# Sixteen units turned by DMA instead of eight, and ScalarE's codes issued up to eight units ahead

## The reference

```
layer 0:  P = softmax(x Wq (x Wk)^T + mask(adj));   x = layernorm(x + P (x Wv))
layer 1:  h = x W^T + b
          e[i, j] = leaky_relu(h[i] . a1 + h[j] . a2 + b_a, 0.2)
          A = softmax(where(adj > 0, e, -9e15));    x = layernorm(x + A h)
```

## Time and profile before

| | |
|---|---|
| median of three runs | 245.96 us (245.84 to 246.24) |
| the profiled execution | 246.06 us, span 244.3 us |
| busy: TensorE, VectorE, ScalarE, GpSimd | 227.7, 185.9, 154.6, 63.4 us |
| DMA | 73.85 MB, mean 302 GB/s, 385 GB/s in most slices up to 165 us |
| granted clock | 1.00 up to 239.6 us |

### The profile page before, as it was taken

The page is one execution under the profiler, slowest core; times in us unless marked ns, Lnnn a source line. Parts: engine busy times, 40 slices in busy tenths (PEclk is TensorE's granted clock), DMA queues, the critical chain, the costliest instruction groups (busy, mean ns, idle before and its releaser), DMA issues.

```text
span 244.3 us, 3945 instructions
## 1 busy us (share of the span) xinstructions
PE 227.7 (93%) x1445; PEld 127.0 (52%) x1445; DVE 185.9 (76%) x284; ACT 154.6 (63%) x182; POOL 63.4 (26%) x107
## 2 busy tenths in 40 slices
PE   3869999999999999999999999999999999999970
PEld 2745666455555556455555545565455555544550
DVE  1378788886998776979677787977877778899352
ACT  3287986989769977640789993710899991420041
POOL 3375578999500000003120000002300000042241
PEclk9999999999999999999999999999999999999996
DMA  5999999999999999999979999999489997310102
GB/s 149 367 383 370 385 386 387 384 386 387 384 387 386 385 387 386 385 384 386 349 167 362 387 396 395 387 386 369 137 295 343 389 256 147 66 51 15 43 3 91
DMA packets 52600, 73.85 MB, mean 302 GB/s; under 512 B 15457, under 2 KB 19810, under 8 KB 52578
## 3 DMA queue, kind: packets, MB, share of 16 engines
q1 hardware_dynamic: 52000, 73.43, 86.4%
q10 hardware_dynamic: 578, 0.13, 0.3%
HBM read 69.36 MB, written 2.10 MB: 293 GB/s over the span
## 4 chain that ended last, share of the span: by engine, by line
PE 85%; POOL 4%; ACT 4%; issue 2%; DMA 1%; DVE 1%; POOLq 0%; DVEq 0%; ACTq 0%
PE banks L1267 68%; PE banks L1218 9%; PE banks L1284 3%; ACT a L792 3%; PE banks L1156 2%; DMA x_sb<-in_x_dram 1%; PE banks L1171 1%; POOL f_parts L682 1%; PE banks L1142 1%; POOL feat L675 1%; POOL rstd L643 1%; POOL f_parts L680 1%; ACT xhat_st L756 0%; POOL xhat_st L648 0%; PE banks L1188 0%
## 5 line engine op out<-in xcount | busy, mean ns | idle before, releaser
L1267 PE MATMUL banks<-e_sb,f_parts 128*128 128x512 f16 (+1 forms) x786 | 183.3, 382 | 1.8 <-DVE e_sb L996 1.2
L984 DVE SCALAR_TENSOR_TENSOR e_sb<-R,cr_word,banks 128x1024 f32<-128x1024 f32 x108 | 133.5, 1275 | 23.5 <-PE banks L1218 20.6
L792 ACT ACTIVATE a<-a_sb,code_bias 128x2048 fp8e4<-128x2048 int32 x64 | 124.8, 1997 | 3.5 <-DMA a_sb<-in_adj_dram 3.0
L1267 PEld LDWEIGHTS banks<-e_sb,f_parts 128*128 128x128 f16 x786 | 72.9, 96 | 86.2 <-issue 1.7
L700 POOL TENSOR_TENSOR frstd<-frv,minus_half 128x4 f32<-128x4 f32 x7 | 8.0, 1149 | 156.5 <-DVE frv L1020 156.5
L1218 PEld LDWEIGHTS banks<-ident,a 128*128 128x128 f16 x432 | 28.2, 97 | 10.3 <-ACT a L792 0.5
L1218 PE MATMUL banks<-ident,a 128*128 128x128 f16 x432 | 32.5, 219 | 0.2 <-ACT a L792 0.2
L779 ACT COPY R<-banks 128x512 f32<-128x512 f32 x8 | 4.7, 587 | 31.7 <-PE banks L1171 31.7
L984 DVE SCALAR_TENSOR_TENSOR e_sb<-R,cr_word,x_sb 128x1024 f32<-128x1024 f32 x16 | 20.5, 1324 | 0.0
L808 ACT ACTIVATE junk<-y 128x128 f32<-128x128 f32 x28 | 8.3, 297 | 19.0 <-DVE y L1011 18.9
L1156 PE MATMUL banks<-m0c_um,x_tr 128*128 128x130 f32 x64 | 9.7, 299 | 1.4 <-ACT x_tr L752 0.7
(11 more groups left out here) (113 smaller groups left out, 108.7 us busy)
## 6 DMA issues: line engine op xcount, KB each, us to landing
a_sb<-in_adj_dram SPq DMA_DIRECT2D x128, 512.0 KB, 10.7
x_sb<-in_x_dram SPq DMA_DIRECT2D x8, 256.0 KB, 8.7
out_dram<-out_sb SPq DMA_DIRECT2D x8, 256.0 KB, 5.9
x_sb<-a SPq DMA_TRANSPOSE x8, 3.4
w_nat<-in_L_gnn_W_dram ACTq DMA_DIRECT2D x1, 64.0 KB, 2.6
wv<-in_L_gnn_Wv_dram ACTq DMA_DIRECT2D x1, 64.0 KB, 3.0
acol<-in_L_gnn_a_vec_dram SPq DMA_DIRECT2D x1, 1.0 KB, 3.1
bcol<-in_L_gnn_b_W_dram ACTq DMA_DIRECT2D x1, 0.5 KB, 2.9
```

The lines of the kernel that those rows point to most:

```text
L792: nc.scalar.activation(a_words[:, n % 2, k, :, Q * h:Q * (h + 1), :].rearrange("p e r x -> p r e x"), a_parts[:, m % SLOTS, :, :].rearrang ...
L984: nc.vector.scalar_tensor_tensor(out=e_sb[:, k % NE, :], in0=R[:, g % 2, :], scalar=cr_word[:, 0, 2 * t + b:2 * t + b + 1], in1=word_codes ...
L1267: ins = nc.tensor.matmul(dst, f[:, j, :], e_half[:, k % NE, cols, part], start=(opened and n == 0), stop=(j == T - 1 and n == 2))
```

## The change

The last sixteen units, the whole fourth group, are transposed by DMA. The ring of eight destinations is used twice: the transfer of unit 56 waits until unit 48's weights are made. The first eight transfers stand between the loads: two of them behind the wait of each of loads 57, 59, 61 and 63 and ahead of its two DMAs. The remaining eight stand behind all loads, as before. From slot 9 on ScalarE's lead grows: slots 9 to 12 issue two codes each (13 and 14, 15 and 16, 17 and 18, 19 and 20), and from slot 13 on codes `slot + 8` stand at the head of each slot. `turned` and `moved` now count over a list of moved units; for these units they give the same as a subtraction.

```diff
-    MOVED = 8
-    CODES_AHEAD = 4
+    MOVED = 16
+    CODES_AHEAD, CODES_LEAD, LEAD_AT = 4, 8, 9
...
+        moved_units = [s for s in range(S) if s >= S - MOVED]
+        turned_units = [s for s in range(S) if s not in moved_units]
         def by_dma(s):
-            return s >= S - MOVED
+            return s in moved_units
         def turned(s):
-            return min(s, S - MOVED)
+            return s - moved(s)
         def moved(s):
-            return s - (S - MOVED)
+            return sum(m < s for m in moved_units)
...
+        def codes_before(slot):
+            return min(slot + min(CODES_AHEAD + max(slot - LEAD_AT, 0), CODES_LEAD), LOADS)
...
                 def move(s):
...
                     if d >= NM:
-                        sp.wait_ge(p_ready, 2 * (s - NM + 1))
+                        sp.wait_ge(p_ready, 2 * (moved_units[d - NM] + 1))
...
                     if m >= SLOTS:
                         sp.wait_ge(codes_ready, m - SLOTS + 1)
+                        if m % 2 == 1 and by_dma(m - SLOTS):
+                            move(m - SLOTS - 1)
+                            move(m - SLOTS)
...
-                for u in range(S - MOVED, S):
+                for u in range(S - SLOTS, S):
                     move(u)
...
-                    if slot + CODES_AHEAD < LOADS:
-                        codes(slot + CODES_AHEAD)
+                    for m in range(codes_before(slot), codes_before(slot + 1)):
+                        codes(m)
...
-                    if s >= NA:
-                        pe.wait_ge(p_ready, 2 * (s - NA + 1))
+                    if m >= NA:
+                        pe.wait_ge(p_ready, 2 * (turned_units[m - NA] + 1))
```

More of the change, by code:

```diff
@@ L538, in load_x, with move @@
                     sp.dma_start(x_pairs[:, i, :, :, :], x_t[:, i, :, :, :]).then_inc(x_loaded[i], 16)
+                def move(s):
+                    n, c = divmod(s, 4)
+                    d = moved(s)
+                    sp.wait_ge(codes_ready, PARTS * n + 2 * (c // 2) + 2)
+                    if d >= NM:
+                        sp.wait_ge(p_ready, 2 * (moved_units[d - NM] + 1))
+                    else:
+                        sp.wait_ge(y0_ready, QUADS)
+                    sp.dma_start_transpose(out=at_moved[d % NM], in_=a16[:, n % 2, c // 2, c % 2, :]).then_inc(
+                        at_landed[d % NM], 16)
                 def load(m):
@@ L971, in edges @@
                     k = 2 * s + b
-                    word_codes = code_moved[moved(s) % NM] if by_dma(s) else ps_code[s % NA]
+                    word_codes = code_moved[moved(s) % NM] if by_dma(s) else ps_code[turned(s) % NA]
                     if b == 0:
@@ L976, in edges @@
                         else:
-                            dve.wait_ge(at_ready, s + 1)
+                            dve.wait_ge(at_ready, turned(s) + 1)
                         if t == 0:
@@ L1212, in turn @@
                         pe.wait_ge(codes_ready, PARTS * n + c + 2)
+                    m = turned(s)
                     if s == 2:
                         pe.wait_ge(r_ready, 2)
-                    if s >= NA:
-                        pe.wait_ge(p_ready, 2 * (s - NA + 1))
+                    if m >= NA:
+                        pe.wait_ge(p_ready, 2 * (turned_units[m - NA] + 1))
                     for r in range(TG):
-                        ins = nc.tensor.transpose(ps_at[s % NA][:, r * P:(r + 1) * P],
+                        ins = nc.tensor.transpose(ps_at[m % NA][:, r * P:(r + 1) * P],
                                                   a16[:, n % 2, c // 2, c % 2, r * P:(r + 1) * P], ident16[:, :])
```

## The result

The changed kernel takes 248.64 us (246.57 to 249.71, 18 runs) against 245.84 us (245.33 to 246.95, 18 runs) for the kernel before: a ratio of 1.0103, 95% interval 1.0086 to 1.0121 (the quotient of the two medians is 1.0114). The forecast was 244.3 us with a range of 242.4 to 245.2. It is slower by about 1%, clear of the noise, where faster was forecast. The profiled execution of it took 248.77 us, with a span of 247.0 us against 244.3.

The account below looks back on a forecast made before the run. The prediction took TensorE's own work as the bound. From the profiled 246.06 us it took 3.6 for transposes and added 1.9 for slot 13's wait: 244.4, or 244.3 us against the median 245.96; range 242.4 to 245.2.

Parts of the forecast that it names:

- Part 1: TensorE, slots of units 48 to 55: without their transposes, eight slots save 0.447 us each, 3.6 us in all.
- Part 3: Slot 13: codes moved ahead delay group 1's first copy to R, so TensorE waits 1.9 us (1.4 to 2.4).
- The other four covers: Group 1's second copy, group 0's sums, groups 2 and 3's copies to R: in time, with 1.2 to 3.8 us left.
- Part 2: SyncE, before loads 57 to 63: eight more DMA transposes at 1.28 us each, costed at nothing for the end.
- My reading of unit 48: Codes 49 done at about 160 us, first pair landed by 176, VectorE wants the unit at 180: some 4 us cover.
- The transfers come late: VectorE's wait for unit 48: each us late adds one at the end, 2 us late gives 246.3 us; chance 0.05.
- The clock: Behind 72.4 us, slot 13's pause lets TensorE's clock fall, adding 3.0 us for 247.3 us; chance 0.08.

Follow-up runs that it names:

- the lead alone: The changed kernel with eight moved units instead of sixteen, so only ScalarE's lead of eight is new against the kernel before: 248.1 us, ratio 1.0095.
- fourteen units above: The kernel with all transposes behind all loads and the lead from slot 17 on, with fourteen moved units instead of twelve: 249.13 us.
- the kernel with twelve behind all loads: The changed kernel with twelve moved units, all transposes behind all loads and the lead growing from slot 17 on: 244.1 us, ratio 0.9937.

## Why the prediction was wrong

**Part 1, right.** Eight slots of 3.157 us become 2.71 us. The rows of after give 3.58 us, the forecast had 3.6. VectorE keeps the pace when it has its units: 4.87 us for two of them, 4.86 in the earlier trace rows.

**Part 3, right in its mechanism, and its size in a single trace.** The wait stands in slot 13, ended by R, for the reason given: 1.29 us in the profiled execution beyond what it lagged before, against 1.9 forecast from the earlier trace rows. The moment was forecast well, R's half at 72.4 and measured at 72.15; the rest of the difference is that TensorE itself came 0.46 us later in this execution. By the lead alone the median cost is 2.3 us, against nothing once the lead starts at slot 17 (ratios 1.0095 and 1.0002). The other four covers held; TensorE's lag is +1.75 in slot 13 and +1.78 in slot 45.

**Part 2, the step that failed.** It read: "Eight more DMA transposes take 1.28 us each of SyncE, and land after 3.2 to 8.3 us on a queue with little on it", and then "Loads 57 to 63 are held up by at most 8 x 1.3 us". The first is the median of the earlier trace rows carried to a place where it does not hold. The row says 1233/1284/3812: its maximum, and the next at 3.2 us, are the two of the eight that had loads and a store in flight ahead of them, and that is where all the transposes stand that the change adds. The term was 10.4 us and measured 29.5. The second error is the one that mattered: I asked whether each transfer and each load would be in time on its own, and not how long one turn of pair, loads, codes and pair would take. A turn took 9 to 13 us for two units (starts at 162.88, 175.76, 185.64, 195.30 and 204.13) where TensorE takes 5.4. The early start covered the first turns, and at slot 56 TensorE lost 3.2 us. My reading of unit 48 was right (codes 49 done at 159.8 us, its transfer landed at 173.8, wanted at 179.95), and it was the wrong unit to look at.

**The rivals.** "The transfers come late" is what happened, with a chance of 0.05, but I placed it at unit 48 and priced it from one landing. The clock was in the list too, with 0.08, behind slot 13. There it did not fall in any profile, after pauses of up to 2.3 us by the idle column; behind the pause of 3.0 us at slot 56 it was 0.50 for 3.4 us and cost 1.7 us, half of its length., from which I took that price, are weak evidence for it, since the granted clock in that trace is 1.00 from 8 to 10 us, where the eight matmuls took 2.07 us; the better row is that of fourteen units above, 36 matmuls in 10.99 us instead of 8.29, the granted clock being 0.50 from 194.8 to 201.6. The two cases belong together: the late transfers made the pause, and the half clock came behind it. The Trainium skill (TensorE: Matmul & The Clock Gate, Part 1: The HAM clock gate) has this rule, that an idle TensorE loses its clock; the trace agrees (0.50 from 213.7 on). In the changed kernel it fell behind the longest wait of the last group, not behind the one that I had priced.

**The sum** with measured terms is 244.3 (span before) + 0.5 (a lag from the start of this execution) + 1.3 (slot 13) - 3.6 (the transposes) + 3.2 (slot 56) + 1.7 (half clock) - 0.4 (a shorter last part) = 247.0, the span after. It is made from the same trace and so must come out; the experiments are what supports its terms.

## What to carry to other kernels

Do not price a transfer by the row's median, but by the rows that have the same traffic ahead of them, and for a DMA transpose ask what will be in flight when it is issued: between loads it costs the backlog, once for each group (8.5 to 9.5 us for the first two of a group of four or more here), and the queue behind it stands still. Where units, codes, loads and transfers depend on one another in a ring, write down how long one turn of the ring takes and set it against the consumer's pace; a lead only moves the start. Put such transfers behind all loads and cut what keeps the loads late; that was worth 1.6 to 2.3 us here against the kernel before, where eight transposes between the loads, with the wait of slot 13, lost 2.8. It has its own edge: with fourteen units and the gather in place it lost 3.5.

## What the runs showed of the hardware

- A DMA transpose of 256 KB on an empty queue takes 1.3 us of the issuing engine and lands after 3.3 us. With loads ahead of it in SyncE's queue the first of a pair lands 0.8 to 1.3 us after the last of them, up to 12.2 us after issue, and the second is taken only when they have nearly landed. A plain copy of the same bytes in the same place lands as late but takes 0.9 us of SyncE, and the loads behind it go out at once.
- A row of transposes with nothing else in the queue came at 1.38 us each (196 to 204 us in the kernel with twelve behind all loads), that is 190 GB/s with the DMA engines busy all the time, where loads came at 385 GB/s. The Trainium skill (Advanced Engine Details and Errata, X-Bar Transpose (TRN2)) has transposes as fast as regular DMAs; here they ran at half the rate of the loads, and the measurement decides.
- From another engine's queue it takes 9.6 to 15.9 us to land, when ScalarE issues it and SyncE the loads, and the second of a pair holds ScalarE for 4.1 to 7.6 us. Why the engines do so, the traces don't show; that transposes and other transfers are kept apart in the DMA engines, or that a transpose's many small packets fill a queue, would both look like this, and it is left open.
- The load behind a gather of 4096 elements of 4 bytes held SyncE for 9.3 us. In the kernel before, a pause of SyncE of 4.8 us stood behind the gather, and no wait of TensorE followed; with the codes ahead the pause is gone. Moving the gather to the end let the transposes begin 2.3 us sooner.
- TensorE's granted clock stayed at 1.00 (2.4 GHz) through pauses of 1.6 and 2.3 us. It was 0.50 (1.2 GHz) for at least 2.4 us behind a pause of 2.8 us, for 3.4 us behind one of 3.0 us, for 6.8 us from within one of 3.9 us on, and for at least 3.4 us behind one of 4.5 us.
